# Two 3x3 convolutions written out over all image pairs, with two sets of padded buffers and the third kernel row in 64x64 tiles

## The reference

```python
def leaky_relu(x): return jnp.where(x >= 0, x, LEAK * x)          # LEAK = 0.01
def conv2d_3x3(x, w, b):                                          # padding 1, NCHW, 64 -> 64 channels
    y = jax.lax.conv_general_dilated(x, w, (1, 1), ((1, 1), (1, 1)), ...)
    return y + b[None, :, None, None]
y = leaky_relu(conv2d_3x3(x, conv_w1, conv_b1))
y = leaky_relu(conv2d_3x3(y, conv_w2, conv_b2))
seq = y.reshape(bN, cN, hN * wN).transpose(0, 2, 1)
```

## Time and profile before

| what | value |
|---|---|
| median of 3 runs | 9213.75 us (9210.48 to 9214.14) |
| the profiled execution | 9213.91 us |
| its span, first to last instruction | 9212.1 us |
| mean granted TensorE clock | 0.967 of full speed |
| first to last MATMUL of line 349 | from 22.97 us to 788.45 us |
| POOL's next work, setup of `pipeline` | 794.13 us |

### The profile page before, as it was taken

One profiled execution on the slowest core, in us unless ns is written; L12 is line 12 of the kernel. 1 busy time (PEld: TensorE's weight loads), 2 busy tenths in 40 slices (PEclk: granted clock), 3 DMA queues, 4 the chain that ended last, 5 costly groups with the idle time before them and its releaser, 6 DMA issues. The chain is left out here.

```text
span 9212.1 us, 136561 instructions
## 1 busy us (share of the span) xinstructions
PE 8300.6 (90%) x39494; PEld 2179.4 (24%) x39494; DVE 7227.8 (78%) x10984; ACT 6259.7 (68%) x12381; POOL 3220.5 (35%) x2315
## 2 busy tenths in 40 slices
PE   7885259999999999999999999999999999999999
PEld 2221012222222222222222222222222222222222
DVE  1114898988888888888898888888898888888821
ACT  1112457777777777777777777777777777777754
POOL 0002443433443434333343344343343434433300
PEclk9997669999999999999999999999999999999999
DMA  5545886777777777767777777777777777777610
GB/s 88 87 81 125 210 203 178 190 179 179 181 182 187 184 184 182 190 174 183 180 185 181 186 180 182 188 182 177 181 185 180 190 179 187 181 177 182 154 30 10
DMA packets 867860, 1529.57 MB, mean 166 GB/s; under 512 B 403304, under 2 KB 436784, under 8 KB 867120
## 3 DMA queue, kind: packets, MB, share of 16 engines
q1 hardware_dynamic: 864048, 1520.67, 68.0%
q10 hardware_dynamic: 3072, 0.40, 0.0%
HBM read 1326.60 MB, written 176.95 MB: 163 GB/s over the span
## 5 line engine op out<-in xcount | busy, mean ns | idle before, releaser
L1227 POOL TENSOR_TENSOR hst<-hst,cbc 128x512 f32<-128x512 f32 x2048 | 2839.3, 1387 | 4640.2 <-ACT carry L983 4019.7
L972 ACT ACTIVATE pr<-bank 128x512 f32<-128x512 f32 x4096 | 2224.0, 597 | 1049.8 <-PE bank L856 944.5
L1120 DVE TENSOR_TENSOR_SCAN hst<-dA,carry,bank 128x512 f32<-128x512 f32 x1792 | 2293.9, 1280 | 64.0
L865 PE MATMUL bank<-pr,vt 128*64 128x512 f32 x8192 | 2212.0, 618 | 0.0
L1062 DVE CUSTOM_DVE_ANT_0 gains<-bank,gains 128x512 f32<-128x512 f32 x2048 | 1405.7, 686 | 855.1 <-ACT gains L920 830.5
L1110 DVE TENSOR_TENSOR bank<-lanes,bbc 128x512 f32<-128x512 f32 x2048 | 1679.6, 820 | 76.8 <-DMA lanes<-spread_d 33.1
L854 PE MATMUL bank<-s1q,s1k 128*128 128x512 bf16 x4096 | 1572.6, 384 | 178.7 <-ACT pr L972 139.4
L978 ACT ACTIVATE dA<-lanes,small 128x512 f32<-128x512 f32 x2048 | 1489.5, 727 | 240.7 <-DMA lanes<-spread_d 149.4
L805 PE MATMUL bank<-s1kx,s1q 128*128 128x512 bf16 x4096 | 1338.8, 389 | 284.8 <-DVE mxp L1062 246.0
L856 PE MATMUL bank<-t2q,t2k 128*128 128x512 bf16 x4096 | 1554.4, 379 | 0.0
L920 ACT ACTIVATE gains<-bank 128x512 f32<-128x512 f32 x2048 | 1234.3, 603 | 188.7 <-PE bank L805 182.4
(11 more groups left out here) (108 smaller groups left out, 6030.5 us busy)
## 6 DMA issues: line engine op xcount, KB each, us to landing
lanes<-spread_d SPq DMA_DIRECT2D x2048, 512.0 KB, 5.3
seqt<-seq_d SPq DMA_DIRECT2D x256, 128.0 KB, 4.5
spread_d<-dsp SPq DMA_DIRECT2D x128, 256.0 KB, 2.0
spread_d<-usp SPq DMA_DIRECT2D x128, 256.0 KB, 2.0
bbc<-bc_d SPq DMA_DIRECT2D x128, 256.0 KB, 3.3
cbc<-bc_d SPq DMA_DIRECT2D x128, 256.0 KB, 3.9
xpad<-in_x SPq DMA_DIRECT2D x64, 256.0 KB, 6.4
ypad<-ypad SPq DMA_DIRECT2D x128, 128.0 KB, 2.8
```

Source lines behind the costliest of these rows:

```text
L865: mm = nc.tensor.matmul(ACC[CH * h:CH * (h + 1), :], vt[:, t, :], pr[:, T % PRING, h, :], start=t == 0, stop=t == KT - 1)
L972: nc.scalar.activation(pr[:, T % PRING, h, :], bank_of(("S", T, h))[:], ACT.Exp).then_inc(S["p_full"], 1)
L1120: nc.vector.tensor_tensor_scan(hst[:, T % HRING, :], dA[:, T % 2, :], DBU[:], carry[:, g:g + 1] if sl % CHUNKS else 0.0, ALU.mult, ALU.add ...
L1227: nc.gpsimd.tensor_tensor(h, h, cbc[:, (T - 1) // GROUPS % 2, :], ALU.mult).then_inc(S["hc_in"], 1)
```

## The change

The hardware loop is written out in Python (`for p in range(PAIRS)`), in one block without barriers between pairs; semaphores count on through all pairs and are cleared once at the end. There are two sets of `xpad` and `ypad`, used by turns (`par = p % 2`). Instead of whole buffers, POOL clears only their edges. SP loads pair 0 as soon as the edges of the first set are clear (`edged` at 2), and issues the 16 loads of pair p + 1 ahead of the moves of pair p. TensorE works on two chunks at a time (a duo, `DUOS = 4` in an image): first the kernel rows 0 and 1 of both chunks as before, 12 matmuls, then the three taps of kernel row 2 as 64-row matmuls in four 64x64 tiles, 12 matmuls. In these, chunk `2j` reads partitions 0 to 63, and chunk `2j + 1` the copy in partitions 64 to 127, one row further up. The weights of kernel row 2 are therefore loaded into both halves, and the zeros are gone. TensorE raises `summed` once for a duo.

```diff
-ROWS_OF = (0, 10, 26, 42, HH)
-NEEDS = {10: 0, 18: 1, 34: 2, 50: 3}
-PASSES = 6
+ROWS_OF = (0, 2 * ROWS + 1, 4 * ROWS + 1, 6 * ROWS + 1, HH)
+DUOS = CHUNKS // 2
...
-        xpad = [sb(f"xpad{i}", [P, PAD, PAD]) for i in range(2)]
-        ypad = [sb(f"ypad{i}", [P, PAD, PAD]) for i in range(2)]
+        xpad = [[sb(f"xpad{par}{i}", [P, PAD, PAD]) for i in range(2)] for par in range(2)]
+        ypad = [[sb(f"ypad{par}{i}", [P, PAD, PAD]) for i in range(2)] for par in range(2)]
...
+                        for t in pair:
+                            nc.gpsimd.memset(t[:, 0, :], 0.0)
+                            nc.gpsimd.memset(t[:, HH:PAD, :], 0.0)
+                            nc.gpsimd.memset(t[:, 1:HH, 0:1], 0.0)
+                            nc.gpsimd.memset(t[:, 1:HH, PAD - 1:PAD], 0.0).then_inc(edged, 1)
...
+                for t, w, b, col in ((wtap[0], w1, b1, 0), (wtap[1], w2, b2, 1)):
+                    sp.dma_start(t[0:CH, 0:3, :], w[:, 0:3, :]).then_inc(weights, 16)
+                    sp.dma_start(t[CH:P, 0:3, :], w[:, 3:6, :]).then_inc(weights, 16)
+                    for half in (0, CH):
+                        sp.dma_start(t[half:half + CH, 3:6, :], w[:, 6:9, :]).then_inc(weights, 16)
+                        sp.dma_start(bias[half:half + CH, col:col + 1], b).then_inc(weights, 16)
+                sp.wait_ge(edged, 2)
+                load_pair(0)
+                for p in range(PAIRS):
+                    par = p % 2
+                    if p + 1 < PAIRS:
+                        if p == 0:
+                            sp.wait_ge(edged, 8)
+                        else:
+                            sp.wait_ge(summed, 2 * DUOS * (p - 1) + DUOS)
+                        load_pair(p + 1)
+                    for k in range(CHUNKS):
+                        sp.wait_ge(leaky, 2 * CHUNKS * p + k + 1)
...
+                        sp.dma_start(ypad[par][0][CH:P, high, 1:1 + WW],
+                                     ypad[par][0][0:CH, low, 1:1 + WW]).then_inc(moved[par][k], 16)
...
+                for s in stored:
+                    sp.wait_ge(s, 16 * PAIRS * CHUNKS // 2)
...
+                            first = 2 * CHUNKS * p + CHUNKS * conv + 2 * j
+                            if first >= 8:
+                                pe.wait_ge(plus_bias, first - 6)
+                            if conv:
+
+                                for k in ((0, 1, 2) if j == 0 else range(2 * j + 1, min(2 * j + 3, CHUNKS))):
+                                    pe.wait_ge(moved[par][k], 32 * (p // 2 + 1))
+                            else:
+                                pe.wait_ge(loaded[par][j], 64 * (p // 2 + 1))
...
+                            for h in range(2):
+                                top = (2 * j + h) * ROWS
+                                for dx in range(3):
+                                    for i in range(2):
+                                        nc.tensor.matmul(into[h][i], wtap[conv][:, dx, :],
+                                                         src[i][:, top:top + ROWS, dx:dx + WW],
+                                                         start=dx == 0, stop=False)
+                            for dx in range(3):
+                                for h in range(2):
+                                    o, top = CH * h, (2 * j + h) * ROWS + 2 - h
+                                    for i in range(2):
+                                        mm = nc.tensor.matmul(into[h][i], wtap[conv][o:o + CH, 3 + dx, :],
+                                                              src[i][o:o + CH, top:top + ROWS, dx:dx + WW],
+                                                              start=False, stop=dx == 2, tile_position=(o, CH * i))
+                            mm.then_inc(summed, 1)
...
+                    act.wait_ge(summed, n // 2 + 1)
...
-                        for t in range(PASSES):
-                            dy, dx = t // 3 * 2, t % 3
-                            for i in range(2):
-                                mm = nc.tensor.matmul(
...
-            clear(nc, [*loaded, *moved, summed, plus_bias, leaky, *stored])
-
-        with nc.Fori(0, PAIRS) as p:
-            pair(p)
```

More of the change, by code:

```diff
@@ L269, in sem @@
             return ctx.enter_context(nc.semaphore(name))
-        wtap = [sb("w1tap", [P, PASSES, CH]), sb("w2tap", [P, PASSES, CH])]
+        wtap = [sb("w1tap", [P, 6, CH]), sb("w2tap", [P, 6, CH])]
         bias = sb("bias", [P, 2])
-        xpad = [sb(f"xpad{i}", [P, PAD, PAD]) for i in range(2)]
-        ypad = [sb(f"ypad{i}", [P, PAD, PAD]) for i in range(2)]
+        xpad = [[sb(f"xpad{par}{i}", [P, PAD, PAD]) for i in range(2)] for par in range(2)]
+        ypad = [[sb(f"ypad{par}{i}", [P, PAD, PAD]) for i in range(2)] for par in range(2)]
@@ L276, in convolutions @@
         biased = sb("biased", [P, 2, CHUNK])
         seq = sb("seq", [P, 2, CHUNK])
-        w_in_sem = sem("conv_weights")
-        with nc.Block() as block:
+        weights, edged, summed, plus_bias, leaky = (
+            sem(n) for n in ("conv_weights", "edged", "summed", "plus_bias", "leaky"))
+        loaded = [[sem(f"loaded{par}{j}") for j in range(DUOS)] for par in range(2)]
+        moved = [[sem(f"moved{par}{k}") for k in range(CHUNKS)] for par in range(2)]
+        stored = [sem("stored0"), sem("stored1")]
@@ L335, in _ @@
+                dve.wait_ge(edged, 8)
+                for p in range(PAIRS):
+                    y0, y1 = ypad[p % 2]
                     for n in range(2 * CHUNKS):
                         conv, k = n // CHUNKS, n % CHUNKS
[L337 to L345, removed]
@@ L346, in _ @@
-                        for t in range(PASSES):
-                            dy, dx = t // 3 * 2, t % 3
-                            for i in range(2):
-                                mm = nc.tensor.matmul(
-                                    banks[n % 8][CH * i:CH * (i + 1), :].rearrange("p (h w) -> p h w", w=WW),
-                                    wtap[conv][:, t, :], src[i][:, k * ROWS + dy:k * ROWS + dy + ROWS, dx:dx + WW],
-                                    start=t == 0, stop=t == PASSES - 1)
@@ L353, in _ @@
[L353 to L369, removed]
+                        dve.wait_ge(plus_bias, 2 * CHUNKS * p + n + 1)
                         src = biased[:, n % 2, :]
                         if conv == 0:
+                            if p >= 2 and k == 0:
+                                dve.wait_ge(summed, 2 * DUOS * (p - 1))
@@ L372, in _ @@
                             src = src.rearrange("p (h w) -> p h w", w=WW)
                             nc.vector.scalar_tensor_tensor(
-                                out=ypad[0][0:CH, 1 + k * ROWS:1 + (k + 1) * ROWS, 1:1 + WW], in0=src[0:CH],
+                                out=y0[0:CH, 1 + k * ROWS:1 + (k + 1) * ROWS, 1:1 + WW], in0=src[0:CH],
                                 scalar=LEAK, in1=src[0:CH], op0=ALU.mult, op1=ALU.max)
                             nc.vector.scalar_tensor_tensor(
-                                out=ypad[1][CH:P, k * ROWS:(k + 1) * ROWS, 1:1 + WW], in0=src[CH:P],
+                                out=y1[CH:P, k * ROWS:(k + 1) * ROWS, 1:1 + WW], in0=src[CH:P],
@@ L378, in _ @@
                                 scalar=LEAK, in1=src[CH:P], op0=ALU.mult, op1=ALU.max).then_inc(leaky, 1)
                         else:
-                            if k >= 2:
-                                dve.wait_ge(stored[k % 2], 16 * (k // 2))
+                            before = (CHUNKS * p + k) // 2
+                            if before:
+                                dve.wait_ge(stored[k % 2], 16 * before)
                             nc.vector.scalar_tensor_tensor(out=seq[:, k % 2, :], in0=src, scalar=LEAK, in1=src,
@@ L383, in _ @@
                                                            op0=ALU.mult, op1=ALU.max).then_inc(leaky, 1)
-            clear(nc, [*loaded, *moved, summed, plus_bias, leaky, *stored])
-        with nc.Fori(0, PAIRS) as p:
-            pair(p)
+        clear(nc, [*loaded[0], *loaded[1], *moved[0], *moved[1], *stored, weights, edged, summed, plus_bias, leaky])
 def pipeline(nc, banks, seq_d, scratch, w_in, cw, cb, w_dt_t, w_dt, dt_b, w_bc, a_log, skip,
```

39 lines of the change are left out of this document (added).

## The result

The changed kernel takes 9006.22 us (median of 4 runs, 9004.28 to 9007.69) against 9212.6 us (9210.48 to 9214.14) for the kernel before: a ratio of 0.9775, interval 0.976 to 0.9789. The forecast was 8992 us, range 8970 to 9040.

A forecast was written before the change was run, and what follows sets the result against it. TensorE bounds the convolution stage, with 12.6 us gaps between pairs. Pair 0 to 99.6, six pairs 401.4, last pair 64.2, plus tail: 566.1 against 788.45 us, saving 222.3; forecast 8992 us, range 8970 to 9040.

The forecast's parts named there:

- rival 1: Small prices: full drain at shape changes, 9003 us; clock falling in the wait, 9002 to 9008; lost steps, 9005; chance 0.19.
- the likeliest case: The forecast as it stands for the whole kernel: 8992 us, 222.3 us saved; chance 0.60.
- TensorE's work: Convolution matmuls: a duo takes 5.15 + 2.57 + 0.30 = 8.02 us, a convolution of a pair 32.1 instead of 41.4.
- The change of shape: TensorE switching tile shape twice in a duo: 0.15 us each, 0.30 a duo.
- The full drain of rival 1: At each tile shape change: 0.30 us, 0.60 a duo, giving 9003 us; part of rival 1's chance of 0.19.
- rivals 3 and 4: Four tiles run two by two, duo 10.6 us, 9130 us, chance 0.11; or one by one, 15.8, 9456, chance 0.02.
- The pair boundary: Between pairs: the 12.6 us gap goes; moves queued behind loads make convolution 2's first duo wait 2.7 us.
- A pair takes 34.8 + 32.1 = 66.9 us: Length of a pair: chunks 0 to 2 landed at 34.8 us, then convolution 2 in 32.1; 97.2 before.
- The reason against it, a short wait after 30 solid microseconds: Argument that TensorE's clock would not fall in the 2.7 us wait ahead of convolution 2.
- The sign that was named, a granted clock of 1.00 through the stage: Expected in the profile after the change: TensorE's granted clock at 1.00 through the convolution stage.
- The start: Pair 0: TensorE starts at 17.6 us, convolution 1 ends at 52.4, waits 12.9 to 65.3, pair ends at 99.6.
- Rival 2: Moves overtake the loads or loads run faster: no wait, 8970 to 8976 us; chance 0.06.

The follow-up runs named there:

- e5: e1 with kernel rows 0 and 1 of four chunks first, then kernel row 2 of both duos; 8948.97 us, ratio 0.9713 to before.
- e1: The changed kernel with the next pair's 16 loads issued two by two, each two behind one chunk's moves; 8959.58 us, ratio 0.9724 to before.
- e2: The changed kernel with the last two of the 16 loads moved behind the moves of chunk 2; 8978.1 us, ratio 0.9742 to before.
- e7: The changed kernel with eight extra matmuls ahead of the wait for ypad in pairs 1 to 6; 8997.8 us, ratio 0.9766 to before.
- e6: The changed kernel with all loads of x issued by GpSimd's own queue, moves and stores by SP's; 9022.98 us, ratio 0.9791 to before.

## Why the prediction came out as it did

The direction, the mechanism and most terms of the sum held; the time is 14 us above the forecast, 0.16% of the whole. But the measured 9006.2 us is what rival 1 had priced for a clock that falls in the wait (9002 to 9008; 0.19 for all of rival 1) and not the likeliest case (8992; 0.60). Measured on the stage alone, the forecast is 21.5 us short, a tenth of the 222.3 us that were to be saved, and that the total is nearer is in part luck (5 below). By the prediction's own steps:

1. *TensorE's work.* A duo was to take 8.02 us and takes 8.04. Four tiles side by side, taken from two-sided bounds of 2.57 and 5.15 us, measure 2.74 with one change of shape. The change of shape was put at 0.15 us; the duo's two parts are 0.16 and 0.17 us over their 12 and 6 steps, and e5 gives 0.31 for two changes. The full drain of rival 1, reckoned there at 0.30 each, is refuted, and so are rivals 3 and 4: a duo of 10.6 or 15.8 us is nowhere.
2. *The pair boundary.* That the moves queue behind the loads, that only convolution 2's first duo waits, in pairs 0 to 6 and not in pair 7, is what the timeline shows, and e1 confirms the cause by removing it. The loads start 2.6 us into the pair (2.9 said). But chunks 0 to 2 are there 32.8 to 34.1 us after the first load, 33.3 on average, not 31.9. In the trace of before, SyncE issued nothing for 2.4 us behind the sixth move; now the moves of chunks 3 to 5 are issued at its heels. That these take the missing 1.4 us is an argument from the queue, and no run separates it.
3. *The step that was mis-sized: the wait taken at its bare length.* "A pair takes 34.8 + 32.1 = 66.9 us" left out the clock. Six pairs measure (522.54 - 101.95) / 6 = 70.1 us: convolution 2 starts at 35.9 on average instead of 34.8, 6.4 us over six pairs, and its first stretch is 1.4 to 2.8 us longer than 5.37, 12.4 us over six pairs. Rival 1 had this, at 10 to 16 us and as the less likely case; e2 and e7 show that it is the idle time that costs it. The reason against it, a short wait after 30 solid microseconds, was wrong: over 60 solid microseconds went before, and the granted clock fell to 0.50 all the same. The sign that was named, a granted clock of 1.00 through the stage, did not come.
4. *The start.* First matmul at 17.79 us (17.6 said). Its slow first steps cost 1.5 us instead of 2.7; convolution 2 of pair 0 began at 67.7 instead of 65.3, and ended 2.4 us late. Its loads began at 8.40 us as said, so it is the time from the first load to the moves that was short here too.
5. *The rest.* The tail from the last matmul to the second stage's setup grew from 5.7 to 7.5 us, of which 0.7 was in the sum. The second stage was to keep its length of 8418 us and has 8411.5 in the profiled run. Against 21.5 us lost in the stage and 1.1 in the tail this gives 6.5 back, by scatter as far as the study can tell. The sum is the 16.1 us by which the profiled execution, 9007.7, is above 8991.6; the median is 1.5 us lower.
6. *Rival 2*, no wait at all, was priced at 8970 to 8976. As an edit (e1) it is worth more, 8959.6, since the 12 us of pair 0 and the slow clock go with it.

## What to carry to other kernels

When a change shortens the stretch that hides a transfer, look at what stands ahead of that transfer in its queue, and price the wait with the clock that it costs: here two loads fewer in front took 2.7 us off the wait and were worth 4.8. Prefetches that are needed latest should be issued in pieces behind the transfers that are needed next, and not as a block ahead of them. A second DMA queue was no substitute for that order in e6: the engines served both queues packet for packet, and the loads had the large packets.

## What the runs showed of the hardware

- Matmuls of 64 rows in a 2 by 2 grid of 64x64 tiles, fp32, into two banks, run four side by side at the pace of one: 24 instructions of 512 columns in 2.74 us, a step of 0.4285 us being the same as for two 128x64 tiles. A change between these two shapes costs 0.16 us, weight load included. The Trainium skill (TensorEngine Tiling (Array Packing), Key Properties) says that a change of mode drains the engine; the trace agrees that there is a price, about half of the 0.30 us that the prediction had reckoned for a drain with a weight load that nothing hides; what it is made of no run separates.
- TensorE's granted clock went to 0.50 in each of six idle stretches of 3.1 to 4.4 us (changed kernel) and stayed at 1.00 through six of 0.6 to 1.5 us (e2) and one of 1.9 (e6); in the changed kernel and e2 TensorE had worked without a gap for over 60 us before each. The price behind it was 1.4 to 2.8 us. Idle time of 3 to 4 us that can't be removed can be filled: with 3.66 us of matmuls into a bank that was free the clock stayed up, and the stage was 10.8 us shorter.
- A queue with 3.2 KB packets (GpSimd's) and one with 250-byte packets (SyncE's), both with a backlog, were served one packet for one (2091 and 2088 in 42 us) and had 96% and 13% of the engines' time; a 128 KB move took 22.4 us (median of four) instead of 2.8, and one was 21.8 us in the issuing.
